# Reordered loads and first operands in a two-layer graph network kernel on one core

## What is computed

```
# layer 0: two SAGE steps; mean(h) = (segment_sum(h[src], dst)) / max(in-degree, 1)
h   = relu(x @ W_self0 + mean(x) @ W_neigh0 + b0)
s   = h @ W_self1 + mean(h) @ W_neigh1 + b1
y   = layernorm(x + s)
# layer 1: GCN with self loops, degrees of row = src
g   = y @ W.T + b
out = layernorm(y + segment_sum(norm * g[col], row)),  norm = deg^-1/2[row] * deg^-1/2[col]
```

## Time and profile before

| | |
|---|---|
| median of 3 runs | 895.42 us |
| profiled execution | 895.43 us, span 893.7 us |
| TensorE matmuls | 840.7 us busy (94% of the span), 4283 |
| VectorE | 460.1 us busy (51%) |
| ScalarE | 177.8 us busy (20%) |
| GpSimd | 458.4 us busy (51%) |
| granted TensorE clock, mean | 0.974 |
| DMA | 180.54 MB, mean 202 GB/s |

### The profile page before, as it was taken

How to read it: one execution, slowest core, us unless ns; L and a number is a source line. 1 busy time by engine, 2 the same in 40 slices (tenths; PEclk the granted TensorE clock), 3 DMA queues, 4 the chain that set the end, 5 groups by cost and what they waited for, 6 DMA issues and landing times.

```text
span 893.7 us, 10973 instructions
## 1 busy us (share of the span) xinstructions
PE 840.7 (94%) x4283; PEld 715.4 (80%) x4283; DVE 460.1 (51%) x714; ACT 177.8 (20%) x218; POOL 458.4 (51%) x343
## 2 busy tenths in 40 slices
PE   6999999999999996999999998967899999999996
PEld 5888888888988896888888886845679889988885
DVE  6365569000128347886545679435435634455554
ACT  4111140202101114441222113012111212200000
POOL 3217858777777868885887888787200000000000
PEclk9999999999999998999999998978989999999998
DMA  8999664645593352778875775175467767755551
GB/s 312 312 425 336 199 223 109 179 107 150 143 278 96 96 127 57 295 268 282 303 245 209 244 259 150 26 201 149 138 182 257 222 209 224 240 190 198 196 197 53
DMA packets 99481, 180.54 MB, mean 202 GB/s; under 512 B 15474, under 2 KB 75898, under 8 KB 94048
## 3 DMA queue, kind: packets, MB, share of 16 engines
q1 hardware_dynamic: 60144, 124.17, 41.9%
q10 hardware_dynamic: 26896, 40.65, 12.9%
q0 software_dynamic: 12384, 14.95, 7.4%
HBM read 107.08 MB, written 72.43 MB: 201 GB/s over the span
## 4 chain that ended last, share of the span: by engine, by line
PE 52%; POOL 20%; DMA 11%; issue 10%; DVE 5%; ACT 2%; POOLq 0%; SPq 0%; ACTq 0%; DVEq 0%
PE ps L1512 21%; POOL adj_in L628 19%; PE ps L1396 11%; PE ps L1546 10%; PE ps L1529 8%; DMA adj_in<-u 4%; DMA panel_tiles<-adj_in 2%; DMA xin<-s0t_scr 2%; PE ps L1380 1%; DMA wt_scr<-late 1%; DVE stats L987 1%; DVE u L1138 1%; DVE outb L1247 1%; DMA outb<-in_L_gnn_W_neigh 1%; ACT wx L822 1%
## 5 line engine op out<-in xcount | busy, mean ns | idle before, releaser
L628 POOL DMA_INDIRECT adj_out<-loops,idx_out x160 | 244.9, 1531 | 68.9 <-issue 62.8
L628 POOL DMA_INDIRECT adj_in<-mult,idx_in x160 | 197.9, 1237 | 90.4 <-issue 90.4
L1512 PE MATMUL ps<-u 128*128 128x512 f32 x840 | 192.8, 393 | 6.7 <-DVE u L1052 6.7
L1512 PEld LDWEIGHTS ps<-u 128*128 128x128 f32 x840 | 159.2, 190 | 40.1 <-issue 6.9
L1529 PE MATMUL ps<-u,panel_tiles 128*128 128x512 f32 (+1 forms) x400 | 101.9, 417 | 24.5 <-DMA panel_tiles<-adj_in 20.3
L1396 PE MATMUL ps<-wx 128*128 128x512 f32 x480 | 114.3, 396 | 2.7 <-ACT wx L685 1.4
L1529 PEld LDWEIGHTS ps<-u,panel_tiles 128*128 128x128 f32 (+1 forms) x400 | 80.5, 204 | 43.3 <-DMA panel_tiles<-adj_in 21.0
L1424 PE MATMUL ps<-wx 128*128 128x512 f32 (+1 forms) x576 | 109.5, 352 | 1.2 <-ACT outb L728 1.1
L1396 PEld LDWEIGHTS ps<-wx 128*128 128x128 f32 x480 | 90.2, 190 | 22.4 <-ACT wx L685 2.3
L1424 PEld LDWEIGHTS ps<-wx 128*128 128x128 f32 x576 | 94.0, 189 | 16.7 <-ACT outb L728 1.7
L1455 PE MATMUL ps<-wx,u 128*128 128x256 f32 (+5 forms) x640 | 96.3, 312 | 2.2 <-DVE ht L1157 2.2
(11 more groups left out here) (164 smaller groups left out, 730.1 us busy)
## 6 DMA issues: line engine op xcount, KB each, us to landing
left_scr<-u SPq DMA_DIRECT2D x7, 2560.0 KB, 9.5
u<-left_scr SPq DMA_DIRECT2D x7, 2560.0 KB, 9.6
xt_scr<-wx ACTq DMA_DIRECT2D x10, 1024.0 KB, 9.2
u<-xt_scr SPq DMA_DIRECT2D x10, 1024.0 KB, 5.1
wx<-xt_scr SPq DMA_DIRECT2D x16, 512.0 KB, 4.0
adj_in<-u POOLq DMA_DIRECT2D x4, 1600.0 KB, 26.4
adj_out<-u POOLq DMA_DIRECT2D x4, 1600.0 KB, 46.9
wx<-adj_in SPq DMA_DIRECT2D x5, 1280.0 KB, 8.2
```

Of the source, the lines that this page charges most:

```text
L628: pool.indirect_dma_start(table, bass.IndirectOffsetOnAxis(ap=index[0:EP, j:j + 1], axis=0), counts[0:EP, j:j + 1], None, bounds_check=CEL ...
L1512: ins = nc.tensor.matmul(ps[:, product_bank(g, i, p), :], left_op[n % 2][:, p, k, left, :], right_op[n % 2][:, k, right, :], start=(not on ...
```

## The change

Five things differ:

- **Self parts.** The parts of chunks 2 and 3 (m = 16 to 31) go to eight half-width slots of `xin` instead of four. Parts 16 to 23 are issued after sums 13, 13, 14, 14, 15, 15, 16, 16, part m from 24 on after sum m-7. The panel of chunk 3 is issued behind part 23 instead of behind part 19, and the weight block (1, 0) behind part 31 instead of behind part 24.
- **First operands.** The first product's operands are split after block 27 on both engines (before: after 28 and 29 on ScalarE, 29 and 30 on VectorE), and the first difference of the right operands is taken after block 14 instead of 26.
- **u.** In the last product the additions of x and b1 to tiles 8 and 9 and the low splits of u's first half stand ahead of the product's five additions.
- **Banks.** The second mean's tiles use the pairs (1, 2, 0, 1, 2, 0, 1, 2, 0, 2), so that tile 0 has banks 2 and 3, which are free one product earlier.
- **Weight rows.** Row tile k of the GCN weight, from k = 2 on, is loaded behind panel k + 2 instead of behind panel k.

```
     def fetch_slot(m):
+        return fetched[m % 4] if m < 2 * KD else fetched_half[m % 8]
+    def fetch_free(m):
+        return m - 3 if m < 2 * KD else 2 * KD - 3 + m % 8 // 2 if m < 3 * KD else m - 7
 # SyncE, stage 2
                 if m >= 4:
-                    sp.wait_ge(h_sum, m - 3)
-                sp.dma_start(fetched[m % 4][...], s0t_scr[...]).then_inc(s0_in[m % 4], 16)
-                if m in (15, 19):
+                    sp.wait_ge(h_sum, fetch_free(m))
+                sp.dma_start(fetch_slot(m)[...], s0t_scr[...]).then_inc(s0_in[m % 8], 16)
+                if m in (15, 23):
                     load_chunk_1(2 + m // 17)
...
-                if m == 24:
-                    for j in range(4):
-                        sp.wait_ge(s0_stored[j], 16 * 6)
-                    load_block(0, 1, 0)
+            for j in range(4):
+                sp.wait_ge(s0_stored[j], 16 * 6)
+            load_block(0, 1, 0)
 # SyncE, stage 4
-                if t < KD:
+                if t < 2 or t >= 4:
+                    k = t if t < 2 else t - 2
                     if t < 2:
                         sp.wait_ge(right_lo, 12)
                     else:
-                        sp.wait_ge(wt_stored[t % 2], 16 * (t // 2))
-                    sp.dma_start(late[:, t % 2, :], w_gcn[t * P:(t + 1) * P, :]).then_inc(wt_in[t % 2], 16)
+                        sp.wait_ge(wt_stored[k % 2], 16 * (k // 2))
+                    sp.dma_start(late[:, k % 2, :], w_gcn[k * P:(k + 1) * P, :]).then_inc(wt_in[k % 2], 16)
 # ScalarE
                 if m == 27:
                     ...
-                if m == 28:
                     left_high(0)
-                if m == 29:
                     right_high(0)
 # VectorE
-                if m == 26:
+                if m == 14:
                     right_sums(0, 0)
-                elif m == 29:
+                elif m == 27:
                     left_low(0)
-                elif m == 30:
                     right_low(0)
...
+                if n == 13:
+                    for t in (8, 9):
+                        stage_bias(t)
+                        add_self(t)
+                        u1_low(0, (t - 8) * HALF)
                 for p in range(HALF):
...
-                    elif n == 13 and p < 2:
-                        stage_bias(p + 8)
-                        add_self(p + 8)
-                    elif n == 13 and p >= 3:
-                        u1_low(0, (p - 3) * HALF)
 # TensorE
                 if q == "MEAN1" and t < 3:
-                    pe.wait_ge(*summed(1, 6, 0 if t == 0 else HALF - 1))
+                    pe.wait_ge(*(summed(1, 5, 3), summed(1, 6, 0), summed(1, 6, HALF - 1))[t])
+                elif q == "MEAN1":
+                    pe.wait_ge(acc_free, acc_index(q, 7 if t == NT - 1 else t - 3) + 1)
```

More of the change, by code:

```diff
@@ L53, in build @@
     BLOCK_ORDER = (6, 4, 5, 7, 0, 1, 2, 3)
+    MEAN1_PAIRS = (1, 2, 0, 1, 2, 0, 1, 2, 0, 2)
     N0, S0, GCN = range(3)
@@ L210, in build @@
         fetched = [quarter(xin[:, :, :], j) for j in range(4)]
+        fetched_half = [xin[:, :, :].rearrange("p a d -> p (a d)")[:, j * 2 * T:(j + 1) * 2 * T] for j in range(8)]
         g_out = [buf.rearrange("p (n h j) -> p n h j", h=2, j=T)
@@ L229, in acc_pair @@
                 return (1, 3, 0)[t % 3]
-            return (2 * NT + t) % 3
+            return MEAN1_PAIRS[t]
         def acc_index(q, t):
@@ L268, in build @@
         s0_stored = sems("s0_stored", 4)
-        s0_in = sems("s0_in", 4)
+        s0_in = sems("s0_in", 8)
         g_stored = sems("g_stored", 4)
@@ L365, in g_bank, with fetch_slot @@
             return (0, 1, 2, 3, 6, 7)[m % 6]
+        def fetch_slot(m):
+            return fetched[m % 4] if m < 2 * KD else fetched_half[m % 8]
+        def fetch_free(m):
+            return m - 3 if m < 2 * KD else 2 * KD - 3 + m % 8 // 2 if m < 3 * KD else m - 7
         def node_cols(chunk):
@@ L499, in _ @@
                 if m >= 4:
-                    sp.wait_ge(h_sum, m - 3)
-                sp.dma_start(fetched[m % 4][:, 0:CHUNKS[c][1] * T], s0t_scr[d, :, lines(CHUNKS[c])]).then_inc(s0_in[m % 4], 16)
-                if m in (15, 19):
+                    sp.wait_ge(h_sum, fetch_free(m))
+                sp.dma_start(fetch_slot(m)[:, 0:CHUNKS[c][1] * T], s0t_scr[d, :, lines(CHUNKS[c])]).then_inc(s0_in[m % 8], 16)
+                if m in (15, 23):
                     load_chunk_1(2 + m // 17)
@@ L1158, in _ @@
                 dve.wait_ge(h_free, m + 1)
-                dve.wait_ge(s0_in[m % 4], 16 * (m // 4 + 1))
-                nc.vector.tensor_tensor(cell, cell, fetched[m % 4][:, 0:width], ALU.add).then_inc(h_sum, 1)
+                dve.wait_ge(s0_in[m % 8], 16 * (m // 8 + 1))
+                nc.vector.tensor_tensor(cell, cell, fetch_slot(m)[:, 0:width], ALU.add).then_inc(h_sum, 1)
                 if 1 <= d <= n // 2:
```

## The result

| | before | change |
|---|---|---|
| median | 895.26 us (4 runs, 893.49 to 896.77) | 866.57 us (4 runs, 865.92 to 867.15) |
| ratio | | 0.9672, 95% interval 0.9654 to 0.969 |
| profiled execution, span | 895.43 us, 893.7 us | 865.92 us, 864.2 us |
| TensorE matmuls busy | 840.7 us (94%) | 833.4 us (96%) |
| GpSimd busy | 458.4 us | 461.2 us |

The change is faster by 28.7 us. The prediction said 39.1 us, a time of 856.3, and the result lies outside its range of 853 to 863.

A forecast was written before the change was run, and what follows sets the result against it. TensorE, busy 94% of the span, was taken to bound the kernel, with only idle time and slow matmuls winnable. Gains 4.6 + 2.4 + 3.2 + 2.3 + 26.6 = 39.1 us gave span 854.6, time 856.3 us; range 853 to 863.

The forecast's parts named there:

- GpSimd doesn't move with it: Gather's start: outbound scatters keep their times, panel lands at 640.9, within 0.7 us of the path, at no cost.
- the scatters bind: Rival at the gather's start: outbound scatters and panel end later than TensorE's path, at 645.7; 860.4 us, chance 0.13.
- h's end: From h's last blocks to the first product: VectorE no longer late for block 20's self part, gain 4.6 us.
- the difference beside the scatters: First difference moved to block 14 delays the inbound scatters and last panel: cost 0.8 us, bounds 0 to 1.5.
- The first product's clock: Start of the products: TensorE's clock holds over the shorter stop of about 2.1 us, gain 2.4 us.
- the clock falls at the short stops too: Rival at the products' and second mean's starts: gains of 2.4 and 2.3 us don't come; 861.0 us, chance 0.15.
- Products to second mean: Stop before the second mean shrinks from 4.22 to about 1.0 us, gain 3.2; clock kept there, 2.3 more.
- Panels: Second mean: three stops for panels, slow matmuls after them and overlap of turn and tile, gain 26.6 us.
- the rival in which they come late: Second mean: weight rows come late behind panels and each of six turns waits; above 897 us, chance 0.02.
- that in which half of the stops stays: Second mean: rows, panels and stores share DMA engines, so half of 26.6 us stays; 869.6 us, chance 0.05.

The follow-up runs named there:

- the last kernel: The change with the diagonal on ScalarE's queue, the first difference behind block 23, and table load and square root behind the two high splits: 856.28 us in 9 runs.
- both moves together: The change with the outbound table's diagonal written early from ScalarE's queue and the first difference behind block 23 instead of 14: 857.54 us, later 858.22 us.
- the diagonal moved: The change with the outbound table's diagonal issued early from ScalarE's queue instead of GpSimd's, between inbound and outbound scatters: 857.40 us.

## Why the prediction was wrong

**The step that failed** is in the sum: "GpSimd doesn't move with it", with a panel landed at 640.9 and no cost. (Its terms, 631.62 + 2.6 + 6.4, add up to 640.6.) The panel landed at 649.6. The last scatter started 7.2 us later than in the trace of before (638.85, 631.62), landed after 3.41 us instead of 2.6, and the panel took 7.3 us instead of 6.4. The 7.2 are:

- 1.4 us at the last inbound scatter (317.41, 316.02). The scatter ahead of the difference started 0.2 us earlier than before, the one beside it took 1.85 us longer. The prediction counted a delay there for the inbound panel and forgot that all 160 outbound scatters stand behind the same one.
- 2.05 us in the landing of the diagonal's DMAs (8.12 against 6.07). Before's second profile has 6.9, and the change's 8.63. The weight rows alone, with before's stage 2, have 7.83, so not all of the difference need come from the change. What lengthens it was not found.
- 3.8 us between first and last scatter, 2.2 of them longer scatters and the rest longer stops. One profile of before was taken as a fixed time of GpSimd, while over the kernels run here first to last is 300.4 to 311.6 us; the change's own two profiles, 310.3 and 309.6, lie at the long end both times.

The stop of 5.52 us and the clock behind it (1.9 us) are 7.4 of the 10.3 us missed. Most of the rest, 2.5 us, is on TensorE's own path, where 36.6 came for 39.1. The rival "the scatters bind" named this mechanism, at 0.13 and 860.4: it added 1.8 us for the scatters and 3.0 for the panel, where 7.2 (scatters), 0.8 (landing) and 0.9 (panel) came, and it had no term for the slow clock behind a stop. With a margin of 0.7 us between two chains of 640 us each, this case needed far more than 0.13.

**h's end: 2.8 us instead of 4.6.** The chain of steps was right and two sizes in it were not. TensorE began the columns of the last inbound panel at 330.55 instead of 328.09, 2.46 us later. The panel was issued 1.4 us later, where the sum had 0.8 for the difference beside the scatters (bounds 0 to 1.5), and took 1.1 longer to land, where the sum took the 9.4 of one profile as fixed (8.9 to 10.7 over ten). The other steps hold: ScalarE's left split ended at 346.62 where they gave 344.0, VectorE's last one at 351.68 where they gave 349.35, both late by about the panel's 2.46, of which the sum had 0.8. The scatter beside the difference took 3.04 us instead of 1.19, and one beside the left low split of 2.83 us took 3.73. The Trainium skill (SBUF — State Buffer, Who interferes with whom) infers that a tensor_tensor does not hold back the generation of descriptors; by these rows it does. Both scatters end 1.06 us after VectorE's operation (308.13 and 307.07; 350.54 and 349.48), and so does the one of 2.72 us in the earlier trace rows. So the cost depends on where the scatter begins, and 0.8 was a fair size for it: 0.7 in five of seven profiles, 1.85 in the change's. As to the self parts, which the prediction put first here, the run with only them undone shows the same stop of 1.4 us without their new order.

**The first product's clock: right.** The products took 2.2 us less (forecast 2.4), at a clock of 1.00 after a stop of 1.42 us. That clocks survive such stops is no rule, though: in the last kernel one of 1.43 us was followed by 0.91, and with h's end undone one of 1.90 by 0.87, while 1.99 us with both moves together left it at 1.00. So the rival "the clock falls at the short stops too" was wrong here and is possible elsewhere.

**Products to second mean: 2.7 us instead of 3.2, the clock 2.6 instead of 2.3.** VectorE was done with the low splits at 542.58, just as TensorE ended the products (542.59), so the stop should have been zero by the prediction's cause. It was 1.55, and 1.3 to 2.2 in the other kernels with this order. The profile names a sum of the last product as what ended it, though the first tile's matmuls read nothing of that product's sums. What the prediction left out is a branch in TensorE's own queue, `pe.If(general > 0)` ahead of `mean1`. The rows give its duration in ns and its start, before and in the change:

```profile
L1590 PEldq COMPARE_BRANCH  x1: 6034/6034/6034, 543.4 to 543.4; - x1
L1598 PEldq COMPARE_BRANCH  x1: 5599/5599/5599, 538.4 to 538.4; - x1
```

Before, it ended at 549.43, hidden behind the wait for the low split (551.69). In the change it ended at 543.96, 1.4 us after the products and the split, and the second mean began 0.17 us behind it. In all thirteen profiles with the new order the mean begins 0.17 to 0.24 us behind the end of this branch; in the five profiles with the old order it begins 0.15 us behind the split, and more than 2 us behind the branch. In all eighteen profiles the branch ends 1.5 us after a packet of 16 KB on the queue named `instruction` has landed (542.48 in the change), which points at a load of instructions as what it waits for; no run moved the branch to prove it. The branch of before already stood 1.8 us behind the products' end (547.61), so its trace could have told that the stop would not shrink to 1.0.

**Panels: right.** 26.5 us for a forecast of 26.6. The stop of 0.8 us at the second turn stayed, as said. Rows landed in time for every turn, so the rival in which they come late is out, and so is that in which half of the stops stays.

**The sum of the parts is right where nothing binds behind them.** Alone, or undone with the diagonal moved, the parts gave 25.6 (weight rows), 7.7 (h's end with its clock; forecast 7.0) and 4.2 us (u and banks; 5.5 on TensorE's path, as forecast), 37.5 in all. With the diagonal moved the kernel is 37.6 below its before, and 1.1 us above the 856.3 of the prediction.

## What to carry to other kernels

When a long chain on another engine ends within a microsecond of the new path, its end in one profile is not a bound: take its spread from several profiles, follow every moved operation through all that stands behind it on that engine, and give the crossing a chance to match. A stop on TensorE costs more than its length when the clock falls behind it (5.52 us cost 7.4 here). When a wait is taken away, look for what the engine's own queue holds behind it, branches too: here one was hidden for 1.8 of 4.22 us. And once two chains meet, look for what holds the hidden one up for no reason: a wait for two small DMAs, which another queue could have issued long before, was worth 9 us, while undoing all of the work at h's end changed nothing clear of the noise.

## What the runs showed of the hardware

- GpSimd stops once in 39 outbound scatters, ahead of the 40th, 79th, 118th and 157th, for 2.3 to 8.7 us, with nothing named as its releaser. The first of them is the longest in most profiles, and differs between two executions of before (7.57 and 5.42 us), hardly between two of the change (8.70 and 8.66).
- Two DMAs of 640 elements of 4 bytes each, beside a panel of 1280 KB, took 6.1 to 8.6 us to land after their issue, and the panel 8.9 to 10.7 instead of 6.1 to 8.1.
- A scatter of 1.19 us is held by a VectorE tensor_tensor of 2.3 to 2.8 us with both inputs in SBUF until 1.06 us after that operation's end, and takes up to 3.8 us.
- TensorE stood for a branch in its queue until 1.4 us after its last matmul (543.96; 542.59), though the operands of the next one were ready.
